# A cross-attention and expert-FFN kernel whose order of work is redrawn on all engines

## The reference, cut to what matters

```python
def gat_layer(x, adj, W, a_self, a_neigh, b):          # 8 heads of 64
    feat = jnp.einsum('nf,hfo->hno', x, W)
    e = leaky_relu(attn_self[:, :, None] + attn_neigh[:, None, :])
    e = e + MASK_VAL * (1.0 - adj)[None, :, :]          # MASK_VAL = -1e10
    alpha = softmax(e, axis=-1)
    out = einsum('hnm,hmo->hno', alpha, feat) + b       # heads side by side
    return elu(out)
...
# xattn: h = gat_layer(ctx, adj, W0 ...); y = gat_layer(h, adj, W1 ...), adj = layernorm(x)
# ffn:   4 experts, row n goes to expert n % 4: down(silu(gate) * up)
x = x + xattn(ctx_512, layernorm(x))                    # x 4 x 512 x 512, ctx 4 x 512 x 128
x = x + ffn(layernorm(x))
```

## Time and profile before

| | |
|---|---|
| median of 3 runs | 215.83 us (214.19 to 215.94) |
| profiled execution, its time | 215.22 us |
| its span | 213.4 us |
| PE busy | 199.7 us, 94% |
| DVE / ACT / POOL busy | 68% / 45% / 50% |
| chain that ended last | PE 70%, DMA 10%, POOL 8%, issue 6% |
| DMA | mean 184 GB/s; 421 GB/s from 10.7 to 16 us, 461 GB/s from 35 to 40 us |

### The profile page before, as it was taken

One profiled execution on the slowest core, in us unless ns is written; L12 is line 12 of the kernel. 1 busy time (PEld: TensorE's weight loads), 2 busy tenths in 40 slices (PEclk: granted clock), 3 DMA queues, 4 the chain that ended last, 5 costly groups with the idle time before them and its releaser, 6 DMA issues.

```text
span 213.4 us, 2755 instructions
## 1 busy us (share of the span) xinstructions
PE 199.7 (94%) x889; PEld 156.6 (73%) x889; DVE 145.3 (68%) x316; ACT 96.1 (45%) x154; POOL 107.5 (50%) x92
## 2 busy tenths in 40 slices
PE   7589999978999989999999999999999999999990
PEld 2137777757887868888888888888888888888860
DVE  0599998994997556996773977948562492733940
ACT  3799989963984422225142452502542525112100
POOL 4000785589668558888489564110772134207400
PEclk9969999996999999999999999999999999999999
DMA  6999569864468259645986567473499227111034
GB/s 194 335 421 416 85 284 301 331 123 136 122 146 204 90 142 241 92 66 69 334 339 98 78 216 273 172 268 127 154 309 369 104 31 266 50 52 49 0 125 129
DMA packets 14738, 39.18 MB, mean 184 GB/s; under 512 B 2768, under 2 KB 2768, under 8 KB 13680
## 3 DMA queue, kind: packets, MB, share of 16 engines
q1 hardware_dynamic: 11392, 33.84, 45.6%
q0 software_dynamic: 3040, 4.86, 14.4%
q10 hardware_dynamic: 288, 0.26, 0.4%
HBM read 31.08 MB, written 8.92 MB: 187 GB/s over the span
## 4 chain that ended last, share of the span: by engine, by line
PE 70%; DMA 10%; POOL 8%; issue 6%; ACT 2%; SPq 1%; DVE 1%; POOLq 0%; ACTq 0%
PE bank L1919 31%; PE bank L1933 15%; PE bank L1809 6%; PE bank L1880 5%; PE bank L1906 5%; DMA ff_row<-f_table,f_row 4%; DMA ctxT<-in_ctx_t 4%; PE bank L1801 4%; POOL x_sb L906 3%; PE bank L1869 3%; POOL ff_row L894 2%; DMA ctxT<-in_ctx,ctx_from 2%; POOL acts L869 1%; PE bank L1895 1%; ACT bank L1056 1%
## 5 line engine op out<-in xcount | busy, mean ns | idle before, releaser
L1919 PE MATMUL bank<-acts,ring 128*128 128x512 f32 x288 | 68.5, 392 | 0.0
L1919 PEld LDWEIGHTS bank<-acts,ring 128*128 128x128 f32 x288 | 53.5, 188 | 11.0
L849 POOL TENSOR_TENSOR ring<-ring_raw,ring 128x1024 fp32r<-128x1024 f32 x13 | 31.9, 2462 | 33.1 <-ACT ring L1016 23.9
L1809 PE MATMUL bank<-wide,acts 128*128 128x512 f32 x168 | 45.1, 420 | 0.0
L1809 PEld LDWEIGHTS bank<-wide,acts 128*128 128x128 f32 x168 | 31.9, 193 | 9.2 <-issue 2.9
L1933 PE MATMUL bank<-ring,wide 128*128 128x512 f32 x144 | 34.8, 391 | 0.0
L906 POOL DMA_INDIRECT x_sb<-y_table,ff_row x16 | 27.4, 1715 | 7.9 <-DMA ff_row<-f_table,f_row 4.5
L1933 PEld LDWEIGHTS bank<-ring,wide 128*128 128x128 f32 x144 | 26.8, 188 | 5.5
L1016 ACT CAST ring<-ring_raw 128x1024 fp32r<-128x1024 f32 x24 | 24.8, 1048 | 10.6 <-DMA ring_raw<-in_gate_up_t 6.5
L1880 PE MATMUL bank<-ring,first_xnT 128*128 128x512 f32 x96 | 23.4, 395 | 0.0
L1880 PEld LDWEIGHTS bank<-ring,first_xnT 128*128 128x128 f32 x96 | 17.6, 188 | 3.6
(11 more groups left out here) (121 smaller groups left out, 245.6 us busy)
## 6 DMA issues: line engine op xcount, KB each, us to landing
ring_raw<-in_gate_up_t SPq DMA_DIRECT2D x16, 512.0 KB, 7.3
x_sb<-in_x SPq DMA_DIRECT2D x4, 1024.0 KB, 9.4
ring_raw<-in_down_t SPq DMA_DIRECT2D x8, 512.0 KB, 6.8
val<-in_x SPq DMA_DIRECT2D x4, 1024.0 KB
out<-x_sb SPq DMA_DIRECT2D x16, 256.0 KB, 4.7
y_table<-val SPq DMA_DIRECT2D x12, 256.0 KB, 4.6
wide_raw<-in_W_t SPq DMA_DIRECT2D x2, 512.0 KB, 7.2
val<-in_ctx SPq DMA_DIRECT2D x1, 1024.0 KB
```

Of the source, the lines that this page charges most:

```text
L849: nc.gpsimd.tensor_tensor(ring[:, r % RING, LO, :], ring_raw[:, r % RING, LO, :], ring[:, r % RING, HI, :].bitcast(F32), ALU.subtract).the ...
L1809: last = nc.tensor.matmul(bank[Y_BANK[n]][:, :], hT[:, b % 2, c, w, t * P:(t + 1) * P], W1p[:, c, v, :], start=False, stop=(c == KC - 1 an ...
L1919: last = nc.tensor.matmul(bank[(UP_BANK if half else GATE_BANK)[KC * e + c]][:, :], ring[:, r % RING, w, col:col + P], xnT[:, (e - 1) % 2, ...
```

## The change

The calls of all five lists are put in another order and the bank tables with them. No call is added, none removed, and no function is changed. The index steps of batch 3 keep their order among themselves. The lists were drawn by a planner that takes all transfers, POOL's included, as one queue in the order of issue. The diff, cut to the stretches spoken of later:

```diff
-        Z_BANK = (0, 1, 2, 3, 0, 1, 4, 2, 0, 1, 2, 3, 6, 0, 6, 7)
+        Z_BANK = (0, 1, 2, 3, 0, 1, 2, 6, 1, 2, 5, 1, 7, 4, 6, 7)
...
             load_ctx(0)
+            load_b1(0)
             load_w(1)
             load_x(0)
-            load_b1(0)
             load_ctx(1)
...
             store_y(2)
-            load_r(3)
             store_y(3)
+            load_r(8)
             fill(3)
...
+            r_low(0)
             h_low(1, 0)
-            r_low(0)
             h_low(1, 1)
+            h_low(1, 2)
+            r_low(2)
             follow(0, 0)
...
-            follow(0, 2)
-            h_low(2, 0)
             gather(0, 0)
             fetch_ctx(12)
             fetch_ctx(13)
-            r_low(2)
             h_low(2, 3)
...
```

More of the change, by code:

```diff
@@ L944, in _ @@
             fetch_ctx(13)
-            r_low(2)
             h_low(2, 3)
             r_low(4)
+            x2_inverse(0, 0)
+            follow(3, 0)
+            h_low(3, 0)
             follow(1, 0)
-            follow(1, 1)
-            h_low(3, 0)
-            x2_inverse(0, 0)
+            gather(0, 1)
             gather(1, 0)
             h_low(3, 1)
-            gather(0, 1)
+            follow(0, 2)
             follow(3, 1)
-            gather(1, 1)
+            follow(1, 1)
             follow(2, 0)
@@ L960, in _ @@
             gather(2, 0)
+            gather(1, 1)
             scatter(13)
@@ L1231, in _ @@
             first_silu(0)
+            r_high(7)
             first_inner_high(0)
@@ L1234, in _ @@
             turned_xn(0, 2)
+            r_high(8)
             first_inner_high(1)
@@ L1661, in _ @@
             x2_moments(0, 2)
+            normalize(0, 2)
             first_inner_low(0)
-            normalize(0, 2)
             first_inner(1)
+            r_low(7)
             turned_low(0, 2)
-            output(0, 0)
-            r_low(6)
+            first_inner_low(1)
             x2_stats(0, 3)
             x2_moments(0, 3)
+            output(0, 0)
+            normalize(0, 3)
             x2_stats(1, 0)
-            first_inner_low(1)
-            normalize(0, 3)
-            x2_moments(1, 0)
+            first_inner(2)
@@ L1674, in _ @@
             x2_stats(1, 1)
-            x2_moments(1, 1)
-            first_inner(2)
             x2_stats(1, 2)
             turned_low(0, 3)
+            x2_moments(1, 0)
+            x2_moments(1, 1)
+            x2_stats(1, 3)
+            output(0, 1)
+            normalize(1, 0)
             x2_moments(1, 2)
-            x2_stats(1, 3)
             x2_moments(1, 3)
-            normalize(1, 0)
+            first_inner_low(2)
             normalize(1, 1)
-            output(0, 1)
-            x2_stats(2, 0)
@@ L1699, in _ @@
+            x2_moments(2, 0)
+            x2_moments(2, 1)
             first_inner_low(3)
+            normalize(2, 0)
+            normalize(2, 1)
+            x2_stats(2, 2)
+            inner(1, 0)
+            turned_low(2, 0)
             output(0, 2)
-            x2_stats(2, 2)
-            normalize(2, 0)
+            inner(1, 1)
+            inner_low(1, 0)
             x2_moments(2, 2)
             x2_stats(2, 3)
+            turned_low(2, 1)
             x2_moments(2, 3)
-            normalize(2, 1)
@@ L1707, in _ @@
-            r_low(8)
-            inner(1, 0)
-            inner(1, 1)
-            inner_low(1, 0)
-            turned_low(2, 0)
+            output(0, 3)
+            normalize(2, 2)
             x2_stats(3, 0)
-            normalize(2, 2)
+            x2_stats(3, 1)
+            normalize(2, 3)
             x2_moments(3, 0)
-            normalize(2, 3)
-            x2_stats(3, 1)
-            turned_low(2, 1)
+            small_maxima()
+            inner(1, 2)
+            x2_stats(3, 2)
+            inner_low(1, 1)
@@ L1729, in _ @@
             normalize(3, 1)
-            turned_low(2, 3)
-            output(0, 3)
-            inner_low(1, 2)
-            inner(1, 3)
-            x_stats(0, 0)
             x_stats(0, 1)
+            inner_low(1, 3)
+            normalize(3, 2)
+            inner(2, 0)
             x_stats(0, 2)
+            r_low(15)
+            output(1, 0)
             x_stats(0, 3)
-            inner_low(1, 3)
-            output(1, 0)
-            r_low(15)
-            inner(2, 0)
-            normalize(3, 2)
@@ L1743, in _ @@
-            x_stats(1, 0)
-            x_stats(1, 1)
             normalize(3, 3)
             turned_low(3, 0)
+            output(1, 1)
+            turned_low(3, 1)
+            x_stats(1, 0)
+            turned_low(3, 2)
+            inner(2, 1)
+            output(1, 2)
+            x_stats(1, 1)
+            turned_low(3, 3)
             inner_low(2, 0)
             x_stats(1, 2)
-            output(1, 1)
-            output(1, 2)
+            inner(2, 2)
             x_stats(1, 3)
             output(1, 3)
-            turned_low(3, 1)
@@ L2084, in _ @@
             turn_xn(0, 2)
+            pe.wait_ge(y_made, 13)
             first_down(0)
```

605 lines of the change are left out of this document (298 added, 307 removed).

## The result

The changed kernel took 222.74 us in the median of 4 runs (221.2 to 224.01), the kernel before 215.22 in 4 runs beside it (214.19 to 215.94): a ratio of 1.035, with a 95% interval of 1.025 to 1.045. It is slower. I had said 213.0, and 217.0 at the most. Some executions fall into a slower state of the chip; the ratios leave these out, the medians do not.

The account below looks back on a forecast made before the run. PE, busy nearly all the span, bounds the kernel, so only its stops and the clock count: -1.0 - 1.5 + 0.8 - 0.42 - 0.3 = -2.4 us, from 215.2 to 212.8, stated as a median of 213.0; range 210.9 to 217.0.

Parts of the forecast that it names:

- step (3): Before PE's stop ahead of turn_ctx(3): the store of tile 3 takes 3.4 us and lands at 38.7.
- my four releasers: ACT, POOL, the store of tile 3 and the list ctx_from release the stop ahead of turn_ctx(3), 1.0 us shorter.
- The landing of the fetch: Rows of batch 3, ahead of turn_ctx(3): fetch_ctx(13) starts at 43.75 and lands 3.89 us later, at 47.64.
- The clock: Behind PE's stop ahead of turn_ctx(3): with the stop at 1.2 us the clock stays up, saving 1.5 us.
- the first stop: PE's wait of 3.1 us for the second block of ctx: it stays, with the change costed at nothing.
- The new stop at `wait_h_lo(pe, 13)`: Last pieces of layer 1: PE waits 0.8 us for h_low(3, 1), behind gather(1, 0) and its lookup on POOL.
- decides from a landing of 4.8: Rival, chance 0.15: a lookup on POOL holds up the last pieces of layer 1, 217.8 us; landing from 4.8 us.
- The stop of 0.42: PE's wait before turn_xn(0, 1): gather(0, 1) is issued 6.5 us earlier, so the stop goes, saving 0.42 us.
- From 80 us on I found no place where PE has to stop: Late part: no stop; nearest are gate(1, 0) and up(1, 0), under 1 us of cover, 0.6 to 0.7 if late.
- The tail: Last down product, output and store at the kernel's end: the same instructions, no term in the sum.
- The rule against the change: POOL's and SP's transfers use different queues, so a lookup would not stand behind megabytes and lands in 2.3 us.
- the first rival: Lookups land in 2.3 us at both places, so neither new stop exists: -3.7 us, 211.5; chance 0.20.

Follow-up runs that it names:

- e9: Kernel before with only load_x(2), 1 MB, moved behind store_y(1) on SP: 216.62 us against 214.10, ratio 1.013.
- e3: Changed kernel with load_r(8) and the 1 MB copy fill(3) moved behind store_f(1): 221.82 us, ratio 1.041 to the kernel before.
- e2: Changed kernel with load_x(2), 1 MB, moved ahead of the first store of batch 0: 222.01 us against 213.09 of the kernel before.
- e8: Changed kernel with gather(0, 0) behind fetch_ctx(12) and fetch_ctx(13) on POOL: 219.71 us, ratio 1.028 to the kernel before.
- e11: Kernel before with count_flag() moved ahead of output(3, 2) on DVE: 214.36 us, ratio 1.003.
- e5: Changed kernel with count_flag() moved behind output(3, 3), last on DVE: 222.74 us, ratio 1.042 to the kernel before.
- the control: The changed kernel run again without an edit, beside the single edits: 222.49 us, ratio 1.039 to the kernel before.
- e6: Changed kernel with h_low(3, 1) moved ahead of gather(1, 0) on POOL: 221.98 us, ratio 1.036 to the kernel before.
- e16: Changed kernel with gather(0, 0) behind the fetches, first_inner_low(3) and two x2 instructions moved on DVE, h_low(3, 1) ahead of gather(1, 0): 217.33 us, ratio 1.013.

## Why the prediction was wrong

- **The step that failed is the start of `gather(0, 0)`, which I set at 39.7 and which came at 42.49, by the landings of the two transfers that it waits for.** The first is the store of tile 3, step (3). DVE made the tile when I said (issue at 35.21, forecast 35.2). It took 6.4 us, not the 3.4 that I chose between 2.5 and 5.9. I chose near the lower end since two ring blocks had gone from in front of it and "the 1 MB of x issued 6 us earlier has landed". It was issued 5.5 us earlier and took 7.5. The same kind of block before took 6.5, a row that I did not read for this. The edit in before (e9) shows this mechanism alone: 5.9 to 8.8 us, the stop from 2.22 to 4.93. It is not the block of x alone: with the ring block and the copy behind the store out of the way (e3) the store took 4.5.
- **The second transfer, the lookup of `follow(0, 0)`, is not among my four releasers at all**, a term put at nothing without a reason. In the new list it is issued at 32.55 instead of 27.78; it took 8.8 us instead of 6.9 and landed at 41.37. Had the store alone landed at 38.7, the gather would have started near 42.3 all the same (41.37 and 0.9 us), an estimate from this trace. Taking the megabyte from in front of both brought both forward (e2), and the fetches out from behind the gather took the stop to 0.81 us (e8).
- **The landing of the fetch**, taken as 3.89 from a stretch with less traffic, was 5.3. The fetch went out 2.0 us later than forecast (45.72 for 43.75) and landed 1.4 us more slowly; this is 3.4 of the 3.9 us by which the stop was mis-sized (5.1 for 1.2), and the rest is PE, there half a microsecond early.
- **The clock.** I took back 1.5 us; the clock fell as before (0.52). With 0.81 us at this place it stayed up, so the term was right for a stop that short, but the stop was not. I also left out that the clock was at 0.50 behind the first stop of before, so that this stop cost more than its 3.06 us.
- **POOL and the list.** The rest held: POOL was free at 38.3 (forecast 39.7), `ctx_from` came at 40.95 (42.1).
- **The new stop at `wait_h_lo(pe, 13)`**: 1.14 us for 0.8, by the mechanism that I gave. The lookup took 3.9 instead of my 3.4, which is the difference; all of it came 5 us later than forecast (`follow(1, 0)` at 58.13 for 53.15), since PE did. As a rival ("decides from a landing of 4.8") it did not happen. **The stop of 0.42 went, that of 0.81 became 0.34** (forecast 0.5).
- **"From 80 us on I found no place where PE has to stop"** failed with 1.92 us. I named the pair, `first_inner_low(3)` and `up(1, 0)`, but priced it at one DVE instruction (0.6 to 0.7). What stood in front was an instruction that waits for a transfer, and its price is the transfer's landing, 9.7 us. Moving `first_inner_low(3)` out from behind it took the stop away.
- **The tail** was to be the same. It is 1.7 us longer. By the traces of e11 and e5 an early `count_flag()` goes with some 0.5 us of it. The other 1.2 us lie outside the span (2.8 to 3.4 us in runs of the changed kernel, 1.7 to 1.9 before and in every edit of it, SP's whole list included). With `count_flag()` last in the changed kernel they grew to 4.2 and more. **This is open**: it comes with a list other than SP's, and I have not shown which or how.
- **The first stop**, costed at nothing: 1.75 in this trace, 1.9 to 3.5 in those of its edits, 3.06 in before. So my sign of being wrong ("the first wait is not 3 us any more") came, but with the same lists up to the end it was 3.27 in e5: it varies from run to run by more than a term, and says nothing of the order of transfers.
- **The sum.** It gives 212.8 for the profiled execution; with the 0.6 us to the median that is 213.4, not 213.0.
- **The rule against the change.** A lookup of 512 words did not land sooner beside large transfers: 8.8 us here, and with one megabyte taken from in front of it 3.9 instead of 6.9. So the first rival, with 2.3 us at both places, was wrong (the second lookup took 3.9), and a model with one queue was nearer to these rows. The Trainium skill (DMA: Bandwidth & Descriptors, section SWDGE vs HWDGE vs iDMA) has the two kinds of transfer in different queues of an engine that takes turns between them. The traces do not show the small one profiting from it: the megabyte issued at 29.75 had landed at 37.2, the lookup issued behind it at 32.55 only at 41.4, and so it is in before (31.3 and 34.7). One row of e9 leans the other way: a lookup issued at 34.42 landed at 41.1, ahead of a ring block issued 0.6 us before it (42.7). No experiment was made for this question alone.

Of the 3.9% of the control, 1.1 points are the gather in front of the fetches and 1.6 more DVE's two waits for a gather (by the edits, in that order; each ratio is good to about 0.3 to 0.7 points, and the last ran on another chip). Some 0.8 is the part behind PE's last matmul (1.7 us). Where the rest, near 0.4, lies is not shown; the stops that come when one is taken away (e6, e16) are the likely place.

## What to carry to other kernels

An instruction that waits for a transfer costs, for all that stand behind it in its list, what that transfer takes to land beside what is still under way and what is issued right behind it, so look for such instructions ahead of what the bounding engine wants, and price them by the landing, not by their own duration. List every transfer that such an instruction waits for: the one that the trace names ended last, and another may stand 0.2 us behind it. When the stop is gone, look at who waits for the thing that was moved: twice here the same microseconds came back one list further, and only both moves together showed a gain (0.8%). A saving is only as good as the latest of its releasers, so the one with the widest bounds belongs in the range at its upper end.
